# Hybrid attention and mixture kernel on one core: normalised tokens turned by DMA transposes instead of TensorE

## The chip, the cores and the metric

One core of a Trainium2 chip runs the whole program. The metric is the device time of one execution in microseconds (us), median of several runs. The engines are TensorE (PE for its matmuls, PEld for its weight loads), VectorE (DVE), ScalarE (ACT), GpSimd (POOL) and SyncE (SP), which only issues DMAs here.

## The reference

Four layers follow one another on x of shape (2, 2048, 256), each reading a layernorm of x and adding its result to x:

```python
x = x + attn_a(layernorm(x))   # 16 heads of 16, causal softmax attention, q = k = v = the normalised tokens
x = x + ffn(layernorm(x))      # router: mean over the tokens of a batch @ Wr, best 2 of 8 experts
x = x + attn_b(layernorm(x))   # q, k, v projections; scores = exp(-|q-k|^2); softmax(scores) @ v @ Wo
x = x + ffn(layernorm(x))      # same weights as the first ffn
# ffn: out = sum over the 2 chosen experts of weight * (gelu(h @ W1 + b1) @ W2 + b2), F = 1024
```

## The kernel before

x stays in SBUF as 32 tiles of 128 tokens by 256 features, tokens on partitions. A product with float32 accuracy is made of three fp16 products (`split_product`: high by high, high by low, low by high), so every operand is held as two fp16 halves, "high" and "low".

Both mixtures and the distance attention need the normalised tokens with features on partitions. The class `Columns` makes them in **units** of two tiles. There are 48 units: 0 to 15 for the first mixture, 16 to 31 for the distance attention, 32 to 47 for the second mixture. In a stage they are counted from that stage's base; in the distance attention this count is called p. For a unit, VectorE writes the normalised tokens in float32 (`norm`, c_xn), TensorE turns them with four float32 transposes into a PSUM bank (`turn`), ScalarE reads the bank for the high half (`high`, c_xhi), and VectorE reads it for the low half (`low`, c_xlo). Only units 0 and 1 take both halves on VectorE (`high_vector`). A ring of four units holds the result.

Every engine runs its own queue in program order, and the queues meet at semaphores. The stages:

- **Head attention** (to about 520 us). Steps of one or two "units" of scores; ACT takes exp of each. PE turns each finished output (`turn_out`) after VectorE has copied it out of PSUM (`copy_out`). VectorE's extra work is listed by output number i; LAST is the first output of the last head group. At i == LAST + 1 it finds the scales (`scales.finish`) and then runs `copy_out(i)`; at LAST + 3 it normalises units 0 and 1 and makes their halves.
- **Mixture** (`mixture`, run twice): 8 chunks of 512 tokens, 16 steps each (2 experts of 8 slices), 128 steps. A step n is `up(n)`, six matmuls of 512 columns on PE into f_h; gelu on ACT; the two halves f_hh and f_hl on VectorE; and, three steps later, `down(n)`, twelve matmuls of 256 columns. Side work is listed by step in `beside(n)`, identically for all engines: with c the chunk and a the step in it, the two units of the next chunk are normalised, turned and split at a = 7 to 9 and 10 to 12. `up` of a chunk's first step waits for that chunk's units. In chunk 0 the weights' halves are made along the way, one part a step, and `up(4)` waits for part 4.
- **Distance attention** (`distance_attention`): 8 chunks of 16 steps, 128 steps. A step is `scores(n)` (six matmuls of 512), d_dist on VectorE, two exp on ACT, the halves d_phi and d_plo on VectorE and `weighted(n - 4)` (twelve matmuls of 256). The table `AT` lists side work by step: norm, turn, values, project, lengths.
- SP issues loads: in a mixture the second batch's expert weights once its router has chosen (step 37), and in the last mixture the stores of the result.

Of the kernel before, what the change touches and what calls it, by code (L numbers as in the profile page):

```python
# [39 lines left out]
P = 128  # L40
# [390 lines left out]
def head_attention(pr, block, distance_inputs, cols, weights, mix, moving, fixed):  # L431
# [8 lines left out]
    with ExitStack() as ctx:  # L440
# [104 lines left out]
        def _(sp):  # L545
# [25 lines left out]
            mix.load_weights(sp, 0, chosen, range(len(mix.PIECES)))  # L571

        @block.vector
        def _(dve):
# [93 lines left out]
            for i, (G, c) in enumerate(outputs):  # L668
# [130 lines left out]
        def _(pe):  # L799
# [7 lines left out]
            def last_group(at):  # L807
# [172 lines left out]
class Columns:  # L980

    RING = 4

    def __init__(self, pr, ctx):  # L990
        sb = pr.sb(ctx)
        self.pr = pr
        self.xn = sb("c_xn", [P, self.RING, D], F32)
        self.hi = sb("c_xhi", [P, KD, self.RING * 2 * P], F16)
        self.lo = sb("c_xlo", [P, KD, self.RING * 2 * P], F16)
        self.s_xn, self.s_turn, self.s_hi, self.s_lo = pr.sems("cols", "xn", "turn", "xhi", "xlo")
# [5 lines left out]
    def at(self, u):  # L1002
        return slice((u % self.RING) * 2 * P, (u % self.RING + 1) * 2 * P)

    def chunk(self, u):

        return slice((u % self.RING) * 2 * P, (u % self.RING) * 2 * P + CHUNK)

    def norm(self, dve, u):
        pr = self.pr  # L1010
        if u >= 2:
            dve.wait_ge(self.s_turn, u - 1)
        for i in range(2):
            b, t = divmod(2 * u % (NB * TILES) + i, TILES)
            dve.tensor_scalar(self.xn[:, (2 * u + i) % self.RING, :], pr.x[:, b * TILES + t, :], pr.mv[:, b, t, 0:1], pr.rstd[:, b, t:t + 1],  # L1015
                              ALU.subtract, ALU.mult).then_inc(self.s_xn, 1)
# [9 lines left out]
    def high(self, act, u, bank):  # L1026
        act.wait_ge(self.s_turn, u + 1)
        act.activation(self.hi[:, :, self.at(u)], bank.rearrange("p (k n) -> p k n", k=KD), ACT.Copy, scale=self.scale(u))\
           .then_inc(self.s_hi, 1)

    def high_vector(self, dve, u, bank):
        dve.wait_ge(self.s_turn, u + 1)
        dve.tensor_scalar(self.hi[:, :, self.at(u)], bank.rearrange("p (k n) -> p k n", k=KD), self.scale(u), None, ALU.mult)\
           .then_inc(self.s_hi, 1)

    def low(self, dve, u, bank):
        dve.wait_ge(self.s_hi, u + 1)
        dve.scalar_tensor_tensor(out=self.lo[:, :, self.at(u)], in0=bank.rearrange("p (k n) -> p k n", k=KD), scalar=self.scale(u),
                                 in1=self.hi[:, :, self.at(u)], op0=ALU.mult, op1=ALU.subtract).then_inc(self.s_lo, 1)
# [172 lines left out]
def mixture(mix, block, loaded, last_layer, finish_ahead, banks_read, tiles_read, all_read):  # L1212
# [6 lines left out]
    with ExitStack() as ctx:  # L1219
# [19 lines left out]
        steps = [(q, c, e, j) for q in range(NB) for c in range(CHUNKS) for e in range(TOPK) for j in range(FT)]  # L1239
        def beside(n):  # L1240
# [5 lines left out]
            if not (last_layer and last_batch and c == CHUNKS - 1):  # L1246
# [914 lines left out]
```

## Time and profile before

| | us |
|---|---|
| median of 3 runs | 1654.05 (1653.84 to 1654.17) |
| the profiled execution, its own time | 1654.1 |
| its span in the trace | 1652.4 |
| PE busy in the span | 1607.8 (97%) |
| VectorE busy | 1069.2 (65%) |
| ScalarE busy | 987.2 (60%) |
| GpSimd busy | 358.9 (22%) |

The span runs from the first to the last instruction of the trace. Busy times overlap, so they do not add up. A share near 100% says which engine may bound a stage; the waits say whether it does.

### The profile page before, as it was taken

What the parts mean: (1) busy time and instruction counts of PE and PEld (TensorE: products, weight loads), DVE (VectorE), ACT (ScalarE), POOL (GpSimd) and SP (SyncE); (2) the same over time, 40 slices, a digit from 0 to 9 for tenths busy, and PEclk for the clock granted to TensorE, in tenths of its full rate; (3) what the DMA queues carried; (4) which work ended last, traced back from release to release, by engine and by line L of the source; (5) the groups of instructions that cost most, each with busy time, mean ns of one, the idle gap of its engine ahead of it and who ended that gap; (6) DMA issues with size and microseconds to landing.
All of it is one profiled execution on the core that took longest, in us unless ns stands there. A gap on an engine that the chain in (4) does not pass through costs nothing.

```text
span 1652.4 us, 30850 instructions
## 1 busy us (share of the span) xinstructions
PE 1607.8 (97%) x11947; PEld 891.8 (54%) x11947; DVE 1069.2 (65%) x2159; ACT 987.2 (60%) x1260; POOL 358.9 (22%) x466
## 2 busy tenths in 40 slices
PE   6999999999999999999999999999999899999998
PEld 2222222222233666666675666666666566666666
DVE  7533454454335975785557688868898887576554
ACT  6999999999998433433336554555445443353332
POOL 3022122122021000000005445544444300000000
PEclk9999999999999999999999999999999999999999
DMA  4013235100030003000000000000000200300000
GB/s 135 20 28 115 77 116 166 23 15 17 20 110 1 1 1 103 1 1 1 1 1 1 1 1 2 1 1 2 1 1 27 77 1 1 128 13 14 13 13 26
DMA packets 44335, 52.92 MB, mean 32 GB/s; under 512 B 3664, under 2 KB 39071, under 8 KB 44191
## 3 DMA queue, kind: packets, MB, share of 16 engines
q1 hardware_dynamic: 44190, 50.96, 9.8%
q8 instruction: 96, 1.57, 0.4%
q14 instruction: 49, 0.39, 0.1%
HBM read 38.88 MB, written 4.19 MB: 26 GB/s over the span
## 4 chain that ended last, share of the span: by engine, by line
PE 66%; ACT 16%; issue 11%; DVE 6%; DMA 0%; POOL 0%; ACTq 0%; DVEq 0%; SPq 0%; POOLq 0%
ACT a_probs L781 15%; PE f_ypsum L1045 7%; PE f_ypsum L1046 7%; PE f_ypsum L1044 7%; PE f_h L1044 7%; PE f_h L1045 7%; PE f_h L1046 7%; PE a_out L539 4%; PE d_outs L1044 3%; PE d_outs L1046 3%; PE d_outs L1045 3%; PE d_banks L1044 2%; PE d_banks L1046 2%; PE d_banks L1045 2%; PE a_scores L919 2%
## 5 line engine op out<-in xcount | busy, mean ns | idle before, releaser
L781 ACT ACTIVATE a_probs<-a_scores 128x1024 f32<-128x1024 f32 x544 | 499.9, 1208 | 8.2 <-PE a_scores L919 8.1
L1395 ACT ACTIVATE f_gelu<-f_h,f_bcol,s_more 128x512 f32<-128x512 f32 x256 | 199.0, 778 | 398.0 <-PE f_h L1046 386.3
L539 PE MATMUL a_out<-a_probs,a_values 128*32 128x512 f32 (+3 forms) x2560 | 294.0, 540 | 6.6 <-ACT a_probs L781 5.6
L1450 DVE TENSOR_SCALAR f_hh<-f_gelu,f_gates_scaled 128x512 f16<-128x512 f32 x256 | 136.7, 534 | 196.7 <-ACT f_gelu L1395 195.8
L1904 ACT ACTIVATE d_score<-d_dist,d_nksq,s_more 128x512 f32<-128x512 f32 x128 | 104.1, 813 | 191.8 <-DVE d_dist L2055 190.0
L1045 PE MATMUL f_ypsum<-f_w,f_hh 128*128 128x256 f16 x768 | 209.3, 273 | 0.0
L1046 PE MATMUL f_ypsum<-f_w,f_hl 128*128 128x256 f16 x768 | 209.3, 273 | 0.0
L1044 PE MATMUL f_ypsum<-f_w,f_hh 128*128 128x256 f16 x768 | 209.3, 273 | 0.0
L1452 DVE SCALAR_TENSOR_TENSOR f_hl<-f_gelu,f_gates_scaled,f_hh 128x512 f16<-128x512 f32 x256 | 192.2, 751 | 9.1
L919 PE MATMUL a_scores<-a_moving,a_fixed 64*128 64x512 f16 (+3 forms) x1280 | 184.0, 354 | 9.6 <-ACT a_probs L781 3.7
L795 POOL TENSOR_SCALAR_AFFINE_SELECT a_probs<-a_probs 128x256 f32<-128x256 f32 (+1 forms) x224 | 98.6, 456 | 420.7 <-ACT a_probs L781 412.5
L1941 POOL TENSOR_TENSOR distance_raw<-distance_raw,d_p 128x512 f32<-128x512 f32 x112 | 146.3, 1306 | 178.4 <-ACT d_p L1879 178.2
L1469 POOL TENSOR_TENSOR x<-x,f_b_wide 128x256 f32<-128x256 f32 x64 | 52.9, 848 | 523.6 <-DVE c_xn L1015 523.5
L1044 PE MATMUL f_h<-c_xhi,f_w 128*128 128x512 f16 x384 | 145.6, 379 | 1.3 <-DVE f_w L1122 1.2
L1045 PE MATMUL f_h<-c_xlo,f_w 128*128 128x512 f16 x384 | 145.5, 379 | 0.0
L1046 PE MATMUL f_h<-c_xhi,f_w 128*128 128x512 f16 x384 | 145.5, 379 | 0.0
L919 PEld LDWEIGHTS a_scores<-a_moving,a_fixed 64*128 64x128 f16 x1280 | 49.0, 94 | 173.3 <-ACT a_probs L781 118.7
L1045 PE MATMUL d_outs<-d_vlo,d_phi 128*128 128x256 f16 x512 | 139.6, 273 | 0.0
L1046 PE MATMUL d_outs<-d_vhi,d_plo 128*128 128x256 f16 x512 | 139.6, 273 | 0.0
L1044 PE MATMUL d_outs<-d_vhi,d_phi 128*128 128x256 f16 x512 | 139.6, 273 | 0.0
L618 DVE COPY a_moving<-a_out 128x1024 f16<-128x1024 f16 x31 | 21.4, 692 | 141.5 <-PE a_out L867 141.4
L539 PEld LDWEIGHTS a_out<-a_probs,a_values 128*32 128x32 f32 x2560 | 55.5, 108 | 96.0 <-issue 71.6
(271 smaller groups left out, 2737.9 us busy)
## 6 DMA issues: line engine op xcount, KB each, us to landing
f_raw<-in_L_ffn_W SPq DMA_DIRECT2D x16, 1024.0 KB, 7.6
f_raw<-in_L_ffn_W SPq DMA_DIRECT2D x24, 512.0 KB, 8.8
a_fixed<-a_moving SPq DMA_DIRECT2D x60, 96.0 KB, 2.3
x<-in_L_attn_a_x SPq DMA_DIRECT2D x7, 512.0 KB, 6.0
out<-x SPq DMA_DIRECT2D x7, 512.0 KB, 2.9
f_raw<-in_L_ffn_W SPq DMA_DIRECT2D x12, 256.0 KB, 4.0
a_fixed<-a_moving SPq DMA_DIRECT2D x60, 32.0 KB, 2.0
f_early_raw<-in_L_ffn_W SPq DMA_DIRECT2D x4, 256.0 KB, 3.4
```

Of the source, the lines that this page charges most:

```text
L539: mm = pe.matmul(spare[32 * j:32 * j + 32, i % 2, skip:skip + w], values[:, G % 2, kt + tile, j, :], probs[:, u % UR, j % 2, col:col + w], ...
L781: act.activation(probs[:, u % UR], scores[:, 2 * (u % SR):2 * (u % SR) + 2, :], ACT.Exp, scale=HD ** -0.5)\
L795: pool.affine_select(out=tri, in_=tri, compare_op=ALU.is_ge, fill=0.0, base=0, pattern=[[0, tri.shape[1]], [1, P]], channel_multiplier=-1) ...
L919: mm = pe.matmul(scores[:, 2 * (u % SR) + h, col_of[a]:col_of[a] + w], fixed[G % 2][head, a, k0:k0 + P], moving[G % 2][head, a, q0:q0 + w] ...
L1044: pe.matmul(out, fixed_hi, moving_hi, start=first, stop=False, skip_group_check=shared)
L1045: pe.matmul(out, fixed_hi, moving_lo, start=False, stop=False, skip_group_check=shared)
L1046: return pe.matmul(out, fixed_lo, moving_hi, start=False, stop=last, skip_group_check=shared)
L1395: act.activation(gel[:, n % HR, :], hps[:, n % 2, :], ACT.Gelu, bias=mix.bcol[:, q, FT * e + j:FT * e + j + 1], scale=pr.scales.hidden)\
L1450: dve.tensor_scalar(hh[:, n % HR, :], gel[:, n % HR, :], gate, None, ALU.mult).then_inc(s_hh, 1)
L1452: dve.scalar_tensor_tensor(out=hl[:, n % HR, :], in0=gel[:, n % HR, :], scalar=gate, in1=hh[:, n % HR, :], op0=ALU.mult, op1=ALU.subtract) ...
L1904: act.activation(score[:, n % 2, :], dist[:, n % DR, :], ACT.Exp, scale=pr.scales.distance, bias=nksq[:, b, kt:kt + 1]).then_inc(s_score, 1)
L1941: pool.tensor_tensor(acc, acc, p32[:, n % R, :], ALU.add).then_inc(s_acc, 1)
```

## The change

The four PE transposes of a unit go away. VectorE still writes the normalised tokens; ScalarE now reads these, untransposed in SBUF, for the high half, VectorE for the low half; then SP issues two DMA transposes, one for each half, each of a 128 by 512 fp16 tile in four blocks of 128 by 128. The ring grows from four to eight units. The columns are stored as tile, feature half, token, so that the 512 moving columns of a matmul are four runs of 128, 256 elements apart, where they were one run of 512. Users wait for the DMA's semaphore (`turned`).

The order of work changes with it. In a mixture the side work becomes norm, high, low at steps 1 to 3, 6 to 8 and 11 to 13 of a chunk, two units for each of chunks 0 to 3 and three for each later one; the first mixture thereby also makes the first six units of the distance attention. In the distance attention, units p = 6 and 7 are made at steps 0 to 4, and p = 8 to 12 from step 34 on. Units 0 and 1 are made on VectorE at i == LAST + 1, ahead of `copy_out`. Core of the diff:

```diff
+            for u in range(2):
+                cols.turn(sp, u)                # SP, head attention, behind load_weights
...
                     scales.finish(dve, spare[:, 0, :])
+                    for u in range(2):
+                        cols.norm(dve, u)
+                        cols.high_vector(dve, u)
+                        cols.low(dve, u)
                 if i == LAST + 2:
...
                 if i == LAST + 3:
-                    cols.norm(dve, 0)
-                    cols.norm(dve, 1)
                     mix.gate(dve, 0)
-                    for u in range(2):
-                        cols.high_vector(dve, u, spare[:, 0, :])
-                        cols.low(dve, u, spare[:, 0, :])
...
-                elif at in (26, 28):
-                    free(0)
-                    cols.turn(pe, (at - 26) // 2, spare[:, 0, :])
-                    reads[0].append((cols.s_lo, (at - 26) // 2 + 1))
...
-    RING = 4
+    RING, PARTS = 8, 2
...
-        self.hi = sb("c_xhi", [P, KD, self.RING * 2 * P], F16)
+        self.tokens_hi = sb("c_tokens_hi", [P, 4, D], F16)
+        self.hi = sb("c_xhi", [P, self.RING * 2, KD, P], F16)
...
-    def turn(self, pe, u, bank):
-        pe.wait_ge(self.s_xn, 2 * u + 2)
-        out = bank.rearrange("p (k n) -> p k n", k=KD)
-        for i in range(2):
-            for k in range(KD):
-                mm = pe.transpose(out[:, k, i * P:(i + 1) * P], self.xn[:, (2 * u + i) % self.RING, k * P:(k + 1) * P], self.pr.ident[:])
-        mm.then_inc(self.s_turn, 1)
+    def high(self, act, u):
+        act.wait_ge(self.s_xn, 2 * u + 2)
+        if u >= 2:
+            self.turned(act, u - 2)
+        act.activation(self.tokens_hi[:, self.place(u), :], self.xn[:, self.place(u), :], ACT.Copy, scale=self.scale(u))\
+           .then_inc(self.s_hi, 1)
...
+    def low(self, dve, u):
         dve.wait_ge(self.s_hi, u + 1)
+        if u >= 2:
+            self.turned(dve, u - 2)
+        dve.scalar_tensor_tensor(out=self.tokens_lo[:, self.place(u), :], in0=self.xn[:, self.place(u), :], scalar=self.scale(u),
+                                 in1=self.tokens_hi[:, self.place(u), :], op0=ALU.mult, op1=ALU.subtract).then_inc(self.s_lo, 1)
+
+    def turn(self, sp, u):
+        sp.wait_ge(self.s_lo, u + 1)
+        for to, of in ((self.hi, self.tokens_hi), (self.lo, self.tokens_lo)):
+            sp.dma_start(to[:, self.tile(u, 0):self.tile(u, 2)].rearrange("p t k n -> p (t k) n"),
+                         of[:, self.place(u), :].rearrange("p t d -> p (t d)"), transpose=True).then_inc(self.s_col[u % 2], 16)
+
+    def turned(self, engine, u):
+        engine.wait_ge(self.s_col[u % 2], 16 * self.PARTS * (u // 2 + 1))
...
+        def units_in(chunk):
+            first, count = (2 * chunk + 2, 2) if chunk < CHUNKS else (3 * chunk - 2, 3)
+            return [u for u in range(first, first + count) if u < TILES or not last_layer]
...
-                for f, i in {7: 0, 10: 1}.items():
-                    if f <= a <= f + 2:
-                        work.append((("norm", "turn", "low")[a - f], base + (TILES // 2) * q + 2 * (c + 1) + i))
+            for f, u in zip((1, 6, 11), units_in(CHUNKS * q + c)):
+                if f <= a <= f + 2:
+                    work.append((("norm", "high", "low")[a - f], base + u))
...
+            for chunk in range(NB * CHUNKS):    # SP in a mixture
+                for u in units_in(chunk):
+                    turn(u)
+                if chunk == CHUNKS // 2:
+                    chosen = mix.chosen(sp, 1, routing)
+                    mix.load_biases(sp, 1, chosen)
+                    mix.load_weights(sp, 1, chosen, range(len(mix.PIECES)))
+                if last_layer and chunk >= 1:
+                    store((chunk - 1) * TPC, TPC)
...
-            turn(2)                             # PE, start of the distance attention
             free_ahead(pe)
-            turn(3)
```

## Rows read from the trace of the kernel before

**Rows 1.** The profile page: busy us, share of the span, instructions of each engine.

```profile
PE 1607.8 (97%) x11947; PEld 891.8 (54%) x11947; DVE 1069.2 (65%) x2159; ACT 987.2 (60%) x1260; POOL 358.9 (22%) x466
```

**Rows 2.** Busy time by stretch: length, engines, clock (1.00 full), DMA share, GB/s.

```profile
478.00:495.00 17.00, 17.00 (x124) 5.57 (x123) 6.58 (x13) 14.54 (x17) 3.34 (x7) 1.00 0.25 86
520.00:862.00 342.00, 341.11 (x2376) 229.98 (x2377) 240.12 (x470) 128.56 (x178) 32.15 (x41) 1.00 0.04 13
862.00:1300.00 438.00, 429.36 (x2925) 287.10 (x2924) 356.74 (x655) 231.70 (x363) 200.02 (x164) 1.00 0.01 4
1190.00:1240.00 50.00, 48.10 (x329) 31.46 (x327) 49.41 (x78) 22.66 (x34) 20.18 (x17) 1.00 0.00 1
1310.00:1652.40 342.40, 336.04 (x2344) 229.29 (x2342) 226.19 (x413) 123.51 (x170) 23.36 (x28) 1.00 0.10 33
```

**Rows 3.** Timeline of PE around one turn: start, us, instruction.

```profile
543.97 0.60 PE L1023 MATMUL f_side<-ident,c_xn 128*128 128x128 f32 x4
544.40 0.38 PE L1044 MATMUL f_h<-c_xhi,f_w 128*128 128x512 f16 x1
544.62 0.38 PE L1045 MATMUL f_h<-c_xlo,f_w 128*128 128x512 f16 x1
```

**Rows 4.** Instructions that read c_xn on PE: ns min/median/max, first and last start.

```profile
L1023 PE MATMUL f_side<-ident,c_xn x120: 272/273/273, 544.0 to 1591.0; 128*128 128x128 f32 x120
...
L1023 PE MATMUL d_turns<-ident,c_xn x60: 272/273/328, 872.5 to 1243.6; 128*128 128x128 f32 x60
...
L1023 PE MATMUL d_banks<-ident,c_xn x4: 272/272/273, 872.1 to 872.4; 128*128 128x128 f32 x4
```

**Rows 5.** End of the head attention: timelines of DVE and ACT, one line of the chain.

```profile
476.37 0.69 DVE L626 COPY a_osb<-a_out 128x512 f32<-128x512 f32 x1
...
478.00 0.59 PE a_out L890 x4
...
479.85 0.48 DVE L1551 TENSOR_SCALAR wq_hi<-distance_raw,s_more 128x512 f16<-128x512 f32 x1
...
481.03 0.48 DVE L1551 TENSOR_SCALAR wk_hi<-distance_raw,s_more 128x512 f16<-128x512 f32 x1
...
494.89 5.61 ACT L781 ACTIVATE a_probs<-a_scores 128x1024 f32<-128x1024 f32 x6 [1.69 <-PE a_scores L919]
...
501.74 1.38 DVE L1015 TENSOR_SCALAR c_xn<-x,mv,rstd 128x256 f32<-128x256 f32 x4
```

**Rows 6.** Start of the first mixture: part 4 of the weights on DVE, up(4) on PE.

```profile
530.13 0.74 DVE L1122 SCALAR_TENSOR_TENSOR f_w<-f_raw,s_all,f_w 128x512 f16<-128x512 f32 x1
...
530.93 0.39 PE L1044 MATMUL f_h<-c_xhi,f_w 128*128 128x512 f16 x1
```

**Rows 7.** The same place in the second mixture.

```profile
1311.18 0.75 DVE L1122 SCALAR_TENSOR_TENSOR f_w<-f_raw,s_all,f_w 128x512 f16<-128x512 f32 x1 [0.20 <-ACT f_w L1113]
...
1311.99 0.39 PE L1044 MATMUL f_h<-c_xhi,f_w 128*128 128x512 f16 x1 [1.24 <-DVE f_w L1122]
```

**Rows 8.** Start of the distance attention: chain (two lines), DVE, PE.

```profile
885.27 1.03 DVE c_xn L1015 x2
...
890.68 0.73 DVE c_xn L1015 x2
...
898.36 0.69 DVE L1038 SCALAR_TENSOR_TENSOR c_xlo<-d_turns,c_xhi 128x512 f16<-128x512 f32 x1 [0.82 <-ACT c_xhi L1028]
...
915.46 0.38 PE L1044 MATMUL d_outs<-c_xhi,wk_hi 128*128 128x512 f16 x1
```

**Rows 9.** DMA: the SP queue's packets and share; an SBUF-to-SBUF copy, us to landing.

```profile
q1 hardware_dynamic: 44190, 50.96, 9.8%
...
a_fixed<-a_moving SPq DMA_DIRECT2D x60, 96.0 KB, 2.3
```

**Rows 10.** Groups of ACT: high half from PSUM, and a like one from SBUF.

```profile
L1113 ACT ACTIVATE f_w<-f_raw,s_all 128x512 f16<-128x512 f32 x48 | 34.1, 711 | 4.2 <-DMA f_raw<-in_L_ffn_W 4.2
...
L1028 ACT ACTIVATE c_xhi<-f_side 128x512 f16<-128x512 f32 x30 | 17.9, 597 | 29.0 <-PE f_side L1023 29.0
```

More of the change, by code:

```diff
@@ L1371, in do @@
             def do(kind, what):
-                if kind == "turn":
-                    cols.high(act, what, side[:])
+                if kind == "high":
+                    cols.high(act, what)
                 elif kind == "tanh":
@@ L1629, in distance_attention @@
               25: [("lengths", 7)],
-              44: [("norm", 8)],
-              45: [("norm", 9)],
-              47: [("turn", 8)],
-              48: [("norm", 10)],
-              49: [("turn", 9)],
-              50: [("norm", 11)],
-              51: [("turn", 10)],
-              52: [("turn", 11)],
-              53: [("project", 8, 0), ("norm", 12)],
+              34: [("norm", 8)],
+              35: [("high", 8)],
+              36: [("low", 8)],
+              38: [("norm", 9)],
@@ L1639, in distance_attention @@
+              39: [("high", 9)],
+              40: [("low", 9)],
+              42: [("norm", 10)],
+              43: [("high", 10)],
+              44: [("low", 10)],
+              46: [("norm", 11)],
+              47: [("high", 11)],
+              48: [("low", 11)],
+              50: [("norm", 12)],
+              51: [("high", 12)],
+              52: [("low", 12)],
+              53: [("project", 8, 0)],
               54: [("values", 8), ("project", 8, 1), ("norm", 13)],
-              55: [("lengths", 8), ("project", 9, 0)],
@@ L1641, in distance_attention @@
-              56: [("values", 9), ("project", 9, 1)],
-              57: [("turn", 12), ("project", 10, 0), ("lengths", 9)],
+              55: [("lengths", 8), ("project", 9, 0), ("high", 13)],
+              56: [("values", 9), ("project", 9, 1), ("low", 13)],
+              57: [("project", 10, 0), ("lengths", 9)],
               58: [("values", 10), ("project", 10, 1), ("norm", 14)],
-              59: [("turn", 13), ("lengths", 10), ("project", 11, 0)],
-              60: [("values", 11), ("project", 11, 1), ("norm", 15)],
@@ L1646, in distance_attention @@
-              61: [("turn", 14), ("project", 12, 0), ("lengths", 11)],
-              62: [("values", 12), ("project", 12, 1)],
-              63: [("turn", 15), ("lengths", 12)],
-              64: [("values", 13), ("project", 13, 0)],
+              59: [("lengths", 10), ("project", 11, 0), ("high", 14)],
+              60: [("values", 11), ("project", 11, 1), ("low", 14)],
+              61: [("project", 12, 0), ("lengths", 11)],
+              62: [("values", 12), ("project", 12, 1), ("norm", 15)],
@@ L1658, in distance_attention @@
               105: [("norm", 16)],
-              106: [("norm", 17)],
-              107: [("turn", 16)],
-              109: [("turn", 17)],
+              106: [("high", 16)],
+              107: [("low", 16)],
+              109: [("norm", 17)],
+              110: [("high", 17)],
+              111: [("low", 17)],
               117: [("tanh",)],
@@ L1724, in _ @@
         def _(sp):
+            free_ahead(sp)
+            for p in range(6, TILES + 2):
+                if p >= cols.RING:
+                    sp.wait_ge(s_v, p - cols.RING + 1)
+                    g = (p - cols.RING) // 2
+                    sp.wait_ge(s_p, KD * (max(task["q", g], task["k", g]) + 1))
+                cols.turn(sp, BASE + p)
             chosen = mix.chosen(sp, 0, routing)
@@ L1886, in weights_high @@
                 mix.part_high(act, 0, i)
-            do = {"turn": high, "values": values_high, "project": project_high, "tanh": tanh, "weights": weights_high}
+            do = {"high": high, "values": values_high, "project": project_high, "tanh": tanh, "weights": weights_high}
             act.activation(rden[0:1, 0, 0:1], pr.ones[0:1, 0:1], ACT.Exp).then_inc(s_table, 1)
@@ L1953, in _ @@
                         add_squares(what[0])
-                    if kind == "norm" and what[0] < BASE:
+                    if kind in ("add", "norm") and what[0] < BASE:
                         add_bias(what[0])
@@ L1963, in low @@
             def low(p):
-                cols.low(dve, BASE + p, turn_bank("turn", p))
+                cols.low(dve, BASE + p)
             def values_low(p):
```

133 lines of the change are left out of this document (58 added, 75 removed).

## The prediction

> **What bounds the kernel now.** I began with the page: PE is busy 97% of the span, no other engine above 65% [rows 1]. An average over stages doesn't say what a PE instruction is worth, so next I read busy time by stretch [rows 2]. In the first mixture PE is busy 341.1 of 342 us, in the second 336.0 of 342.4 including its tail; VectorE is at 70% and 66% there. In the distance attention PE has 429.4 of 438. The clock is full everywhere. Third, the timeline around a turn, to see whether PE's work there is back to back: the four transposes start at 543.97, the next matmul at 544.40 and the one after at 544.62 [rows 3], so a turn takes 0.43 us out of PE's stream (the 0.60 of its row overlaps its neighbour). What PE does not have to do in these stretches comes off the time. There are two exceptions. In 1190 to 1240 VectorE is busy 49.4 of 50 us and PE waits, but no turn lies in it. And the head attention mostly goes by ACT's exp, with one stretch, 478 to 495, in which PE is busy 17.0 of 17.0 us and ACT only 14.5 [rows 2]: there a stall of PE is lost time.
>
> **Removed from PE.** The turns are counted from the transposes [rows 4]: 120 + 60 + 4 = 184, four to a turn, so 46 turns after 520 us (16 in the first mixture, 16 in the distance attention, 14 in the second). 46 x 0.43 = 19.8 us. The two turns of the head attention lie beside ACT's exp and are worth nothing. Two places need a look. The 2 turns of steps 107 and 109 come behind the stretch where VectorE is the bound, and PE waits at times in steps 3 to 7 of the distance attention, where 4 turns lie; if neither gave anything, 6 x 0.43 = 2.6 us less would be saved.
>
> **Added on ACT and VectorE in the steady steps.** ACT's high half read PSUM in 597 ns; a like operation from SBUF takes 711 [rows 10]: 0.11 more, on an engine busy 128.6 of 342 us [rows 2], so nothing. VectorE's low half stays a two-input pass over 128x512; it moves within queues that have a quarter to spare. ACT no longer waits for PE's turn but for the norm, which is one step earlier. Hidden, unless VectorE is more than about one step late.
>
> **Moved: units 0 and 1 on VectorE, ahead of a copy.** This is the cost I find in the queues. At LAST + 1 the new block stands between `scales.finish` and `copy_out`. Before, the copy starts at 476.37, right behind the scales, takes 0.69, and PE's `turn_out`, which waits for it, starts at 478.00 [rows 5], 0.94 after the copy's end. The block: two norms of a unit cost half of 1.38, so 0.69 a unit; a high and a low half from SBUF take 1.18 (from wq_hi at 479.85 to wk_hi at 481.03) [rows 5]. 2 x (0.69 + 1.18) = 3.7 us. Queued behind it are `copy_out` and `finish_out` on VectorE; PE waits for the copy, 3.7 - 0.94 = 2.8 us, and behind PE's wait stand the products and scores that ACT needs. From 478 PE is the bound until ACT is fed again at 494.89, after waiting 1.69 [rows 5], and from there ACT is; so the stall passes to the end. Bounds: 0 if PE finds slack that busy time hides, 3.7 if none of the 0.94 covers it. I take +2.8. What is saved at LAST + 3 lies in VectorE's idle time.
>
> **Moved: the first unit's norm to step 1 of a chunk.** In chunk 0 of both mixtures it now stands before part 4 of the weights in VectorE's queue, and `up(4)` waits for that part. First mixture: part 4 is made at 530.13 in 0.74 and PE starts at 530.93 [rows 6], so there is no slack; a norm (0.65 to 0.73 for two tiles) delays PE by 0.65. Second mixture: part 4 starts at 1311.18 after 0.20 idle and PE has waited 1.24 for it [rows 7]; 0.65 - 0.20 = 0.45 more. Together +1.1 (bounds 0 and 1.4). Later steps of chunk 0 have VectorE catching up, so nothing more.
>
> **Added: 96 DMA transposes.** No transfer before is a transpose. Nearest below: an SBUF-to-SBUF copy of 96 KB lands in 2.3 us [rows 9]. By packets: 9.8% of 16 engines' span for 44190 packets is 0.059 us each [rows 9]; 128 partitions by 4 blocks as packets of 256 bytes are 512 packets, 512 x 0.059 / 16 = 1.9 us. Two transposes of a unit then take T = 2 x 1.9 + 2.3 = 6 us. If instead every 2-byte element were a packet, one transpose would take 65536 x 0.059 / 16 = 240 us. I take 6, since the copy row is the nearest. The cover: in a mixture a step is 342 / 128 = 2.7 us, less the turns 2.6; a chunk's second unit has its low half at step 8 and is needed at step 16, about 21 us. `high` and `low` wait for the transposes of two units ago, ten steps. SP has little else; the second batch's weights now wait behind unit 7 (steps 38 to 41) and are not used before step 56. The tightest place is p = 7 in the distance attention: its low half comes in step 4, where before unit p = 5 had it at 898.36, and `project` needs it where PE stood at 915.46 [rows 8], less four removed turns, 913.7. That is 15 us for one T. p = 6 is split in step 2, some 1.5 us behind the 890.68 row, so both must fit into 913.7 - 892.2 = 21.5 us: T up to 10.7 costs nothing.
>
> The Trainium skill (VectorE: DVE Perf Modes, The three transpose paths) gives 1309 ns for a DMA transpose of 128x128; eight blocks one after another are by that page 10.5 us, an estimate, which would leave the sum as it is. No row here shows it.
>
> **Start of the distance attention.** VectorE and ACT carry the chain here, with c_xn at 885.27 (1.03) and 890.68 (0.73) in it [rows 8]. Four of six units go elsewhere, but what remains is packed into steps 0 to 4, with norms, a low half and POOL's adds earlier. I see up to 3 us either way, and count only PE's turns.
>
> **Sum.** -19.8 + 2.8 + 1.1 = -15.9 us. The profiled execution took 1654.1, of which 1652.4 is span; it stands at the median of the runs (1654.05). 1654.1 - 15.9 = **1638.2 us**, 1.0% faster.
>
> **Rivals.**
>
> 1. *The stall at LAST + 1 does not reach the end, or the distance start gains more.* For: the four units that leave that chain. Against: PE at 17.0 of 17.0. Worth 2.8 to 5.8 less: 1632.5 to 1635.5.
>
> 2. *The transposes come too late: slower.* Place: p = 7. Over T = 13.9 us, three units a chunk of 16 x 2.61 = 41.8 us no longer fit, and the backlog of twelve units from chunk 4 on meets p = 6 and 7. Chunk 4 starts four chunks before the mixture's end at 867.1, so at 699.9; the first low half is 7.8 us later; p = 7 lands at 707.7 + 14 T and is due at 913.7. The loss is 14 T - 206 us. It cancels the gain of 15.9 from T = 15.8; with T = 20 it is 74 us: 1712. For it: no row shows a transpose, and element-wise packets would be far beyond. Against: the copy row.
> The Trainium skill's same page (Rules for kernel authors) says to transpose 128x128 on TensorE if PSUM will do as a destination; by that rule the change would be for the worse, and this rival is how.
>
> 3. *The moving operand in four runs of 128 columns slows the matmuls.* 1536 + 192 = 1728 matmuls read it, one each 0.216 us (544.40 to 544.62). No matmul of before reads separated runs. 9 ns each cancel the gain; doubling them would cost 373 us. Against: the transposes, 128 columns each, come at 0.43 / 4 = 0.11 us, and a break is no new instruction.
>
> 4. *No change:* removed turns uncover other waits. VectorE is at 81% in the distance attention [rows 2]; if none of its 16 turns paid and the other costs stood at their bounds, 30 x 0.43 = 12.9 less 5.1 would still be 7.8 us faster. Same time needs some of rival 2 or 3 as well.
>
> **How the numbers follow.** Forecast 0.62 (own range 1635 to 1643); rival 1, 0.17; between the forecast and no gain, 1643 to 1651, 0.06; no change to 0.2%, about 3.3 us, which is about what a measurement of this kernel can tell, 0.03; rival 2, 0.08; rival 3, 0.04. Faster 0.85, same 0.03, slower 0.12. The range 1632 to 1650 leaves out the slower cases and a little below: about 2 in 10.
>
> **What the profile after would show.** No c_xn on PE; PE's matmul of 512 columns still each 0.216 us; first mixture about 6.9 - 0.65 us shorter, the second 6.0 - 0.45; a wait of PE's a_out transpose for a_osb of about 3 us near 478; DMA transposes landing in about 4 us, and PE never waiting for one. Wrong would be: waits of PE or ACT for a transpose, above all at the start of the distance attention; longer matmuls; or an unchanged distance stage with VectorE near 100%.

## The result, and the profile after

The changed kernel takes 1646.52 us (median of 6 runs, 1646.32 to 1648.1) against 1654.11 us for the kernel before (6 runs, 1652.36 to 1654.31). The ratio is 0.996, 95% interval 0.9948 to 0.9972: 0.4% faster, where 1.0% (1638.2 us) was forecast. The runs of either kernel fall on two levels some 1.8 us apart, five of the six of before on the upper one and four of the six after on the lower, so that within a level the change gains some 6 us and not 7.6, and where the medians of a few runs are compared below, 1.8 us are not told from chance.

The profile page of the changed kernel, the line that answers to [rows 1]:

```profile
PE 1589.9 (97%) x11755; PEld 869.9 (53%) x11755; DVE 1079.5 (66%) x2159; ACT 985.9 (60%) x1260; POOL 360.7 (22%) x466
```

The turns are gone: 192 fewer matmuls, 17.9 us less of PE. But the span fell by 7.8 us only (1652.4 to 1644.6), and VectorE has 10.3 us more to do in the same number of instructions. That second number was not in the forecast. Busy time by stretch, answering to [rows 2] (length, engines, granted clock, DMA share, GB/s):

```profile
478.00:484.00 6.00, 5.14 (x28) 1.02 (x28) 4.34 (x10) 2.33 (x4) 0.00 (x0) 0.72 1.27 220
...
520.00:862.00 342.00, 340.16 (x2364) 226.73 (x2363) 248.36 (x488) 134.39 (x187) 35.25 (x45) 1.00 0.12 29
862.00:1300.00 438.00, 422.83 (x2846) 278.11 (x2845) 365.01 (x643) 228.03 (x356) 202.56 (x164) 1.00 0.05 11
1000.00:1040.00 40.00, 38.34 (x263) 25.03 (x262) 39.52 (x56) 20.17 (x31) 21.70 (x19) 1.00 0.14 27
1230.00:1255.00 25.00, 21.84 (x152) 14.19 (x151) 24.62 (x35) 12.02 (x20) 11.55 (x8) 1.00 0.12 23
```

To see where the time went I set the two traces side by side by TensorE's own landmarks: the first matmul of a step of the mixture or of the distance attention, and in the head attention ACT's exp of a unit. A stretch between two landmarks holds the same work in both kernels. All in us:

| landmark | before | after | this stretch, after less before | forecast |
|---|---|---|---|---|
| exp 500 of the head attention | 478.26 | 476.33 | -1.93 | 0 |
| exp 510 | 487.76 | 490.24 | **+4.42** | +2.8 |
| mixture 0, last step | 860.40 | 856.90 | -5.99 | -6.9 + 0.65 |
| distance attention, step 8 | 911.55 | 904.72 | -3.33 | -2.6 |
| step 42 | 1017.27 | 1010.44 | 0 | 0 |
| step 72 | 1134.66 | 1129.72 | **+1.89** | -3.4 |
| step 108 | 1238.00 | 1233.09 | +0.03 | 0 |
| step 114 | 1254.74 | 1252.39 | **+2.57** | -0.9 |
| mixture 1, last step | 1640.58 | 1632.83 | -5.41 | -6.0 + 0.45 |

The column of forecasts adds to -15.9, the measured one to -7.75. The -1.93 at the top is older than anything that was changed: the granted clock of 20 to 30 us is 0.83 in the profiled run of before and 1.00 in the one after (1.00 is 2.4 GHz and a stretch at 1.2 GHz counts half). The change itself is worth the other 5.8 us. The two rows, first before, then after:

```profile
20.00:30.00 10.00, 8.06 (x84) 2.73 (x74) 6.94 (x19) 6.39 (x8) 3.52 (x7) 0.83 0.19 49
```

```profile
20.00:30.00 10.00, 9.03 (x102) 3.12 (x99) 8.25 (x28) 8.98 (x10) 3.31 (x7) 1.00 0.23 59
```

Three rows in bold hold the miss: the stall is 1.6 us dearer than forecast, and the two stretches of the distance attention together are 8.8 us worse. There units p = 8 to 17 are made: 8 to 15 in steps 34 to 64, and 16 and 17, the first two of the second mixture, in steps 105 to 111.

**The stall.** The waits of PE in 476 to 490, and PE's timeline behind the wait:

```profile
PE a_out L887 <- DVE a_osb L628: 2.8, 1, 2.8
```

```profile
478.86 0.66 PE L887 MATMUL a_out<-ident,a_osb 128*128 128x128 f32 x4 [2.78 <-DVE a_osb L628]
479.45 1.68 PE L539 MATMUL a_out<-a_probs,a_values 128*32 128x512 f32 x8
```

The wait is the forecast's 2.8 us to the tenth. What it did not have stands behind it: the granted clock is 0.72 in 478 to 484, where it was 1.00 before, and the 8 products take 1.68 us. The same 8 before:

```profile
478.52 1.07 PE L539 MATMUL a_out<-a_probs,a_values 128*32 128x512 f32 x8
```

**The distance attention.** In 1000 to 1040 VectorE is busy 39.52 of 40 us and PE 38.34; in 1230 to 1255 it is 24.62 and 21.84 of 25. The same lines of the kernel before, for 1000 to 1040 and 1235 to 1260:

```profile
1000.00:1040.00 40.00, 40.00 (x280) 27.30 (x279) 33.03 (x55) 19.96 (x31) 23.44 (x20) 1.00 0.00 1
1235.00:1260.00 25.00, 24.97 (x179) 16.93 (x178) 23.32 (x43) 13.41 (x21) 12.30 (x9) 1.00 0.01 2
```

So the bound moved from TensorE to VectorE. PE's waits for VectorE in 980 to 1260, first before, then after, say the same:

```profile
PE d_banks L1044 <- DVE d_dist L2055: 1.8, 4, 0.8
```

```profile
PE d_banks L1047 <- DVE d_dist L2070: 4.7, 10, 0.8
PE d_misc L396 <- DVE pooled L390: 1.8, 1, 1.8
PE d_outs L1047 <- DVE x L2031: 1.2, 1, 1.2
```

Why VectorE is longer is seen by groups; first after, then before, both 980 to 1260, VectorE (busy us, mean ns | idle before):

```profile
L2015 DVE TENSOR_SCALAR d_phi<-d_p 128x512 f16<-128x512 f32 x86 | 54.3, 631 | 0.0
...
L1032 DVE SCALAR_TENSOR_TENSOR c_tokens_lo<-c_xn,c_tokens_hi 128x512 f16<-128x512 f32 x10 | 13.6, 1362 | 0.0
L1013 DVE TENSOR_SCALAR c_xn<-x,mv,rstd 128x256 f32<-128x256 f32 x20 | 12.9, 687 | 0.0
```

```profile
L1996 DVE TENSOR_SCALAR d_phi<-d_p 128x512 f16<-128x512 f32 x87 | 50.7, 583 | 0.0
...
L1015 DVE TENSOR_SCALAR c_xn<-x,mv,rstd 128x256 f32<-128x256 f32 x20 | 10.5, 565 | 0.0
...
L1038 DVE SCALAR_TENSOR_TENSOR c_xlo<-d_turns,c_xhi 128x512 f16<-128x512 f32 x10 | 6.9, 690 | 3.0 <-ACT c_xhi L1028 3.0
```

The low half went from 690 to 1362 ns. It is the same operation on as many elements; its float32 input went from PSUM (`d_turns`) to SBUF (`c_xn`). It is not slow by itself: over the whole kernel its minimum and median are 680 and 684 ns, its maximum 1760. Timelines of VectorE and GpSimd side by side show what the long ones have in common:

```profile
1022.74 1.76 DVE L1032 SCALAR_TENSOR_TENSOR c_tokens_lo<-c_xn,c_tokens_hi 128x512 f16<-128x512 f32 x1
```

```profile
1022.61 1.33 POOL L1960 TENSOR_TENSOR distance_raw<-distance_raw,d_p 128x512 f32<-128x512 f32 x1 [0.80 <-ACT d_p L1900]
```

GpSimd's sum of the softmax denominators began at 1022.61 and ended at 1023.94, 1.20 us after the low half's start; the low half took 1.76 and ended 0.56 us behind it. In the distance attention ten low halves begin under a GpSimd instruction, and nine of them end 0.55 us behind its end. The tenth, at 887.75, took 0.68; there GpSimd's add of a bias took 1.43 us, the longest of its 32 (median 0.83). Passes with one input in SBUF are held too where they write fp16 from float32 (`d_phi`, up to 1.49 us for 0.42) or normalise (`c_xn`, up to 1.37 for 0.40), but not the statistics of x (0.42 at most). The kernel before had a low half and such a sum side by side too, and nothing happened:

```profile
1035.56 0.69 DVE L1038 SCALAR_TENSOR_TENSOR c_xlo<-d_turns,c_xhi 128x512 f16<-128x512 f32 x1 [0.23 <-ACT c_xhi L1028]
```

```profile
1035.12 1.33 POOL L1941 TENSOR_TENSOR distance_raw<-distance_raw,d_p 128x512 f32<-128x512 f32 x1 [0.80 <-ACT d_p L1879]
```

**The transposes** are waited for by nobody. They land in 2.4 and 2.5 us (median), and no wait of PE or ACT ends with one:

```profile
c_xhi<-c_tokens_hi SPq DMA_TRANSPOSE x48, 2.4
c_xlo<-c_tokens_lo SPq DMA_TRANSPOSE x48, 2.5
```

### The profile page after: what moved, and what is told of

Same layout as the page of the kernel before. It is cut to its first block, busy times and chain, and to the rows that moved or that the text cites. A ratio compares the mean times of both kernels' runs of the same rounds, so it can differ in the third digit from the quotient of the medians.

```text
span 1644.6 us, 30645 instructions
## 1 busy us (share of the span) xinstructions
PE 1589.9 (97%) x11755; PEld 869.9 (53%) x11755; DVE 1079.5 (66%) x2159; ACT 985.9 (60%) x1260; POOL 360.7 (22%) x466
## 4 chain that ended last, share of the span: by engine, by line
PE 63%; ACT 16%; issue 11%; DVE 8%; POOL 1%; DMA 0%; ACTq 0%; DVEq 0%; POOLq 0%
ACT a_probs L782 15%; PE f_ypsum L1047 7%; PE f_ypsum L1049 7%; PE f_ypsum L1048 7%; PE f_h L1047 7%; PE f_h L1049 7%; PE f_h L1048 7%; PE a_out L539 4%; PE d_outs L1047 3%; PE d_outs L1049 2%; PE d_outs L1048 2%; PE a_scores L916 2%; DVE d_dist L2070 2%; PE d_banks L1047 2%; PE d_banks L1049 2%
```

## The experiments

The lengths of the stretches, each less that of the kernel before, from each kernel's profiled run (us):

| kernel | start to exp 500 | exp 500 to 510 | mixture 0 | distance 34 to 72 | 72 to 108 | 108 to 114 | 114 to mixture 1 | mixture 1 | span |
|---|---|---|---|---|---|---|---|---|---|
| after | -1.93 | +4.42 | -5.99 | +1.89 | +0.03 | +2.57 | 0.00 | -5.41 | 1644.6 |
| a1 units 0, 1 put back | -0.01 | 0.00 | -6.00 | +1.87 | +0.03 | +2.56 | +1.67 | -5.42 | 1643.8 |
| a2 one unit ahead | -0.24 | +1.00 | -5.99 | +1.84 | +0.01 | +2.55 | 0.00 | -5.42 | 1642.8 |
| a3 weights first | -0.13 | +4.42 | -6.05 | +1.82 | +0.02 | +2.57 | -0.01 | -4.99 | 1646.7 |
| e1 steps 7, 10, 13 | -0.17 | +4.43 | -6.71 | +1.88 | +0.02 | +2.56 | +1.63 | -6.03 | 1646.7 |
| b4 old steps | -0.34 | +4.42 | -5.99 | +2.29 | -0.01 | +1.60 | 0.00 | -5.42 | 1645.6 |
| b1 GpSimd narrow | -1.23 | +4.41 | -5.99 | -2.55 | -3.68 | -0.47 | -3.22 | -5.41 | 1630.8 |
| b2 the same, before | -1.66 | +0.01 | 0.00 | -0.03 | -3.24 | -0.03 | -3.23 | +0.24 | 1644.4 |
| b3 low half narrow | -2.09 | +2.84 | -5.99 | -0.57 | +0.02 | +1.62 | +1.67 | -5.41 | 1641.1 |
| c1 units 8 to 17 by TensorE | -1.71 | +4.41 | -5.99 | -0.02 | +0.01 | 0.00 | +3.31 | -5.42 | 1643.6 |
| d0 new steps, SBUF | -1.87 | +4.26 | -5.99 | +5.95 | +0.05 | +2.56 | +1.69 | -5.41 | 1650.3 |
| d1 new steps, PSUM | -1.62 | +4.38 | -5.99 | -0.11 | -0.68 | -0.30 | 0.00 | -5.41 | 1639.3 |
| f1 all three | -1.63 | +0.01 | -6.62 | -0.11 | -0.69 | -0.29 | +1.67 | -5.59 | 1635.8 |

The start of the distance attention up to step 34 is left out: -3.3 to -3.4 in every kernel with the change. Stretches that an edit doesn't touch repeat to a few hundredths, apart from the first, the stall and the one behind step 114: there the granted clock falls in some executions and not in others.

### a1: units 0 and 1 back in their old place

```diff
                     scales.finish(dve, spare[:, 0, :])
-                    for u in range(2):
-                        cols.norm(dve, u)
-                        cols.high_vector(dve, u)
-                        cols.low(dve, u)
...
                 if i == LAST + 3:
+                    cols.norm(dve, 0)
+                    cols.norm(dve, 1)
                     mix.gate(dve, 0)
+                    for u in range(2):
+                        cols.high_vector(dve, u)
+                        cols.low(dve, u)
```

> Against the changed kernel (1646.5 us), with VectorE's work for units 0 and 1 put back behind the copy_out of LAST + 2, where it stood before the change. Theory 1: the 4.4 us that TensorE loses between probability units 500 and 510 come whole from this block (2.8 us of waiting for a_osb, and some 1.6 us at half the granted clock behind the wait): 4.4 us faster, 1642.1 us, the granted clock stays at 1.0 there and no wait of 2.8 us for a_osb is left. Rival, the linear one that the prediction used: only the wait of 2.8 us goes, 1643.7 us. Rival: what comes free here is waited for again at the first up-projection of mixture 0, since the transposes of units 0 and 1 then start later: 0 us, and a wait for c_xlo at mixture 0's start.

Measured 1644.54 us (4 runs, 1643.52 to 1645.46; ratio to before 0.9946, 0.9929 to 0.9962). The stretch is back at 0.00 and its clock at 1.00, so all 4.42 us belong to the block. The time moved by 2.0 us, not the 4.4 expected. The profiled run pays 1.67 us at the end of the distance attention, where PE waits 1.5 and 2.1 us for VectorE's gates; the changed kernel has the same two waits at full clock, this run fell to 0.72 behind them. The first stretch is 1.92 us longer than in the profiled run of after as well.

```profile
PE d_misc L1207 <- DVE gathered L1203: 2.1, 1, 2.1
PE d_misc L1187 <- DVE f_gates_scaled L1183: 1.5, 1, 1.5
```

```profile
1286.00:1292.00 6.00, 5.53 (x23) 2.90 (x24) 4.00 (x8) 2.67 (x4) 1.53 (x3) 0.72 0.01 4
```

### a2: one unit ahead instead of two

```diff
-                    for u in range(2):
+                    for u in range(1):
                         cols.norm(dve, u)
                         cols.high_vector(dve, u)
                         cols.low(dve, u)
...
                 if i == LAST + 3:
+                    cols.norm(dve, 1)
+                    cols.high_vector(dve, 1)
+                    cols.low(dve, 1)
                     mix.gate(dve, 0)
```

> Only unit 0 stands ahead of the copy_out of LAST + 1, unit 1 behind that of LAST + 2. The block is then some 1.85 us against a slack of 0.94 us. Theory 1 (the clock falls because the wait is long): a wait of about 0.9 us and no fall of the clock, so that units 500 to 510 cost +0.9 us against the kernel before, 3.5 us less than in the changed kernel: 1643.0 us. Rival, linear: half of the loss stays, +2.2 us, 1644.3 us. Rival: the loss has nothing to do with the length of the block: +4.4 us, 1646.5 us.

Measured 1644.53 us (one run). PE's wait for `a_osb` is 1.0 us, the clock stays at 1.00, and the stretch costs +1.00. Half of the block is 1.87 us by the prediction's own rows, less the slack of 0.94 leaves 0.93: the linear count is right for the wait. The rest of the 4.42 is the clock, and another run shows it apart: in b3, whose head attention is that of the changed kernel, PE waited the same 2.8 us, the clock stayed at 1.00, and the stretch cost +2.84.

```profile
PE a_out L890 <- DVE a_osb L628: 1.0, 1, 1.0
```

```profile
478.00:484.00 6.00, 5.28 (x42) 1.58 (x44) 4.20 (x10) 5.33 (x7) 0.00 (x0) 1.00 1.26 284
```

The same window and the wait in b3:

```profile
478.00:484.00 6.00, 5.29 (x42) 1.59 (x44) 4.18 (x10) 3.50 (x5) 0.00 (x0) 1.00 1.18 203
```

```profile
PE a_out L887 <- DVE a_osb L628: 2.8, 1, 2.8
```

### a3 and e1: the mixtures' units behind the weights, or at the old steps

a3 moves the three lines in `beside` that append norm, high and low below the one that appends the weights. e1 is:

```diff
-            for f, u in zip((1, 6, 11), units_in(CHUNKS * q + c)):
+            for f, u in zip((7, 10, 13), units_in(CHUNKS * q + c)):
```

> In the mixtures' side work the norm, the high half and the low half of a unit stand behind the weights' halves of the same step, in place of ahead of them. Theory 1: the +0.99 us at steps 3 to 6 of mixture 0 and the +0.7 us at the start of mixture 1 are weights that VectorE and ScalarE make later by the length of a norm and a high half: both vanish, 1.7 us faster than the changed kernel, 1644.8 us. Rival: they are the transfers of the transposes, or SP's queue, which this leaves alone: 0 us, 1646.5 us.

> The changed kernel with the units of a mixture chunk taken up at its steps 7, 10 and 13 instead of 1, 6 and 11. Theory: the +0.99 us at steps 3 to 6 of mixture 0 and the +0.49 us at the start of mixture 1 come from the norm and high half at steps 1 to 3, beside the making of weights that the next up-projections wait for: both vanish, 1.5 us faster, 1645.0 us. Rival: the transposes, having less lead, are waited for at the next chunk: over 1646.5 us.

a3 measured 1648.39 us and e1 1648.37 us (one run each; in both the first stretch is 1.8 us longer than in the profiled run of after, and e1 lost 1.63 us behind step 114). By the stretches, a3 is 0.06 us better in mixture 0 and 0.42 worse in mixture 1, and e1 gains 0.72 and 0.62, 1.3 us of the expected 1.5. Step by step more can be seen. `up(4)` starts 0.79 us late in mixture 0 of the changed kernel and 0.49 late in mixture 1, both against the kernel before, behind the norm and part 4 in VectorE's queue:

```profile
532.29 0.73 DVE L1013 TENSOR_SCALAR c_xn<-x,mv,rstd 128x256 f32<-128x256 f32 x2
...
533.27 0.88 DVE L1125 SCALAR_TENSOR_TENSOR f_w<-f_raw,s_all,f_w 128x512 f16<-128x512 f32 x1
```

```profile
534.21 0.39 PE L1047 MATMUL f_h<-c_xhi,f_w 128*128 128x512 f16 x1 [0.80 <-DVE f_w L1125]
```

In a3, with part 4 ahead of the norm, it is 0.00 and 0.19: the order is the cause of this part. But a3 pays it back. `up(6)`, which loses 0.20 in either mixture of the changed kernel, loses 0.59 in a3 (its wait is below), and some 0.35 more is lost before step 12. At steps 7, 10 and 13 (e1) neither `up(4)` nor `up(6)` of mixture 0 is late at all.

```profile
541.02 0.39 PE L1047 MATMUL f_h<-c_xhi,f_w 128*128 128x512 f16 x1 [0.43 <-DVE f_w L1125]
```

### b1 and b2: GpSimd's sums narrowed, after and before

```diff
                     pool.wait_ge(s_acc, added[0])
-                    pool.tensor_tensor(acc, acc, p32[:, n % R, :], ALU.add).then_inc(s_acc, 1)
+                    some = slice(0, 64)
+                    pool.tensor_tensor(acc[:, some], acc[:, some], p32[:, n % R, some], ALU.add).then_inc(s_acc, 1)
```

> The changed kernel with GpSimd's accumulation of the softmax denominators narrowed from 512 to 64 columns (but for the first one of each chunk): it leaves out seven eighths of the denominators' sums. Theory 2a: VectorE's passes whose operands all lie in SBUF are stretched while GpSimd works on SBUF. Then c_tokens_lo falls from 1.25 us to about 0.7 us, VectorE is no longer the bound, and the 8.9 us missing in steps 43 to 63 and 109 to 114 come back: 1637.6 us. Rival 2b: the low half is long for its own sake (two float operands out of SBUF): it stays at 1.25 us and the time at 1646.5 us.

> The same cut of GpSimd's accumulation in the kernel before (it leaves out seven eighths of the denominators' sums). Its low halves read PSUM and TensorE is its bound there. Theory 2a: no change beyond 1 us, 1654.1 us, which makes the gain of the changed kernel's twin its own. Rival: GpSimd's accumulation is itself something that the distance stage waits for, and both kernels gain alike.

b1 measured 1632.52 us, b2 1646.14 us (one run each). In the two stretches of units 8 to 17 the changed kernel goes from +4.46 to -3.02, 7.5 us of the 8.8 that were missing; the kernel before doesn't move there (-0.06). The low half:

```profile
L1032 DVE SCALAR_TENSOR_TENSOR c_tokens_lo<-c_xn,c_tokens_hi 128x512 f16<-128x512 f32 x10 | 7.7, 767 | 0.0
```

1362 to 767 ns with not one instruction of VectorE changed. The edit frees the other passes over SBUF too, so the 7.5 us are not the low half's alone. Both kernels also win in 72 to 108 and behind 114, b1 6.9 us against the change and b2 6.5 against the kernel before, where the expectation had put at most 1 us and only its rival had both gain. Up to step 108 VectorE is the bound in 1190 to 1240 [rows 2], and passes over SBUF are held there as well: `d_phi` takes 611 ns in 72 to 108 of the kernel before and 416 in b2. Behind 114 PE waits for VectorE, first before, then in b2 (1250 to 1300):

```profile
PE d_misc L1203 <- DVE gathered L1199: 2.2, 1, 2.2
PE d_misc L1183 <- DVE f_gates_scaled L1179: 1.5, 1, 1.5
```

```profile
PE d_misc L1203 <- DVE gathered L1199: 0.4, 1, 0.4
```

The kernel before had been paying this all along.

### b3: the low half of units 8 to 17 over 64 of 512 columns

```diff
+        part = slice(0, 32 if 24 <= u < 34 else D)
-        dve.scalar_tensor_tensor(out=self.tokens_lo[:, self.place(u), :], in0=self.xn[:, self.place(u), :], scalar=self.scale(u),
+        dve.scalar_tensor_tensor(out=self.tokens_lo[:, self.place(u), part], in0=self.xn[:, self.place(u), part], scalar=self.scale(u),
```

> The changed kernel with the low half of units 8 to 17 of the distance stage made over 64 of 512 columns (it leaves out seven eighths of those low halves); transposes, norms and high halves are left as they are. Theory 2: 1.1 us of VectorE are gone for each of ten units, TensorE is the bound again, and 8.9 us come back: 1637.6 us. Rival: the missing time lies in the transposes (SP, DMA) or in ScalarE's extra 0.6 us for the high half, which all stay: 1646.5 us.

Measured 1642.83 us (one run). 3.4 us come back in the two stretches (+4.46 to +1.05), not the 8.9 expected. The group says why: with an eighth of the columns it still takes 897 ns.

```profile
L1033 DVE SCALAR_TENSOR_TENSOR c_tokens_lo<-c_xn,c_tokens_hi 128x64 f16<-128x64 f32 x10 | 9.0, 897 | 0.0
```

One of the ten began with GpSimd idle and took 215 ns; five took 1291 to 1293. What lengthens it is a wait inside the instruction, whose size does not depend on its own. So an estimate of VectorE's load by elements, mine of 1.1 us saved for a unit included, is wrong here.

### b4: units 8 to 17 at the steps of the kernel before

The rows of the table `AT` for these units are those of the kernel before, each turn replaced by a high and a low half.

> The changed kernel with units 8 to 17 of the distance stage taken up at the steps of the kernel before (norms at 44, 45, 48, 50, 53, 54, 58, 60, 105, 106, both halves at 47, 49, 51, 52, 57, 59, 61, 63, 107, 109), still turned by DMA. Theory 2: in the distance stage VectorE is the bound because its low half (c_xn and c_tokens_hi, both in SBUF) takes 1.25 us where the old one (PSUM) took 0.69 us. Then putting the units closer together helps nothing: between 2 us slower and 1 us faster than the changed kernel, and the low halves still take over 1.1 us. Rival (the placement is at fault, not the length): the 8.9 us that are missing in steps 43 to 63 and 109 to 114 come back, 1637.6 us. Rival (DMA lead): TensorE waits for columns at its projections of steps 53 to 61, and the time is over 1650 us.

Measured 1647.3 us (one run). The two stretches together cost +3.89 instead of +4.46. When the units are taken up makes 0.6 us here. The low halves still take 1324 ns, as expected.

### c1: units 8 to 17 by TensorE again, the others by DMA

```diff
+    def turn_pe(self, pe, u, bank, s_turn):
+        pe.wait_ge(self.s_xn, 2 * u + 2)
+        out = bank.rearrange("p (t k n) -> p t k n", t=2, k=KD)
+        for i in range(2):
+            for k in range(KD):
+                mm = pe.transpose(out[:, i, k, :], self.xn[:, 2 * (u % 2) + i, k * P:(k + 1) * P], self.pr.ident[:])
+        mm.then_inc(s_turn, 1)
```

with both halves reading the bank, at the old steps.

> The changed kernel with units 8 to 17 of the distance stage turned by TensorE into PSUM as before, at the steps of the kernel before, their halves read from the bank; all other units are turned by DMA. Theory 2: these ten units cost 4.35 us of TensorE's turns and win back the 8.9 us: the ledger of steps 42 to 114 is that of the kernel before, 4.5 us faster than the changed kernel, 1642.0 us. Rival: the loss is not tied to where the low half reads: the turns of TensorE come on top, 1650.9 us.

Measured 1644.65 us (4 runs, 1643.74 to 1645.39; ratio to before 0.9945, 0.9929 to 0.9962). Steps 42 to 114 are those of the kernel before to 0.02 us, 4.5 us better than the change. At the end of the distance attention 3.31 us go again, by the same waits and a clock of 0.91 and then 0.68 in the two windows from 1280. Handing these ten units to the DMA queues, with their tokens in SBUF, was worth less than nothing.

### d1 and d0: the normalised tokens in PSUM, and their control

d1 leaves every transpose to the DMA queues and writes the norms of units 8 to 17 into the bank of the values, at steps 33 to 52 (and 105 to 111), where that bank is free. d0 has the same steps with the tokens in `c_xn`.

```diff
+    def rows(self, u):
+        if u in self.IN_BANK:
+            return self.bank.rearrange("p (t d) -> p t d", t=2)
+        return self.xn[:, self.place(u), :]
...
-            dve.tensor_scalar(self.xn[:, 2 * (u % 2) + i, :], pr.x[:, b * TILES + t, :], pr.mv[:, b, t, 0:1], pr.rstd[:, b, t:t + 1],
+            dve.tensor_scalar(self.rows(u)[:, i, :], pr.x[:, b * TILES + t, :], pr.mv[:, b, t, 0:1], pr.rstd[:, b, t:t + 1],
```

> The changed kernel, its transposes all left to the DMA queues, with the normalised tokens of units 8 to 17 of the distance stage written into the PSUM bank of the values instead of c_xn, so that both halves read PSUM; their steps move to 33 to 52, where that bank is free. Theory 2, sharpened by the traces of the narrowed kernels: a VectorE pass whose operands all lie in SBUF and that begins while GpSimd's tensor_tensor runs is held to its end; one with an operand in PSUM is not. Then the low half takes 0.69 us whatever GpSimd does, and with TensorE's turns gone too the 8.9 us missing after step 42 come back: 1637.6 us by the changed kernel's level. Rival (the two norms of a unit, 0.64 us each by the mean, are held as well and are as much to blame): about half comes back, 1642 us. Rival (ScalarE or SP): 1646.5 us.

> The control of the last: the same steps 33 to 52, the normalised tokens in c_xn in SBUF as in the changed kernel. Theory 2: the low halves are held by GpSimd again (1.1 to 1.8 us) and steps 33 to 53 are at least 3 us longer than with the tokens in PSUM: 1644 to 1648 us. Rival (the steps were at fault): the same time as with the tokens in PSUM.

d1 measured 1642.72 us (4 runs, 1641.02 to 1644.49; ratio to before 0.9936, 0.992 to 0.9953), d0 1651.98 us (one run). From step 34 to 114 d1 is at -1.09 and d0 at +8.56: 9.6 us between two kernels that differ in the place of one tile (and in one wait of the norms that goes with it). d0 is 4.1 us worse than the changed kernel in these stretches and above the 1644 to 1648 that was expected: packing the units closer made the loss larger, which b4's 0.6 us had not shown. First d1, then d0, VectorE in 980 to 1260:

```profile
L1022 DVE TENSOR_SCALAR d_turns<-x,mv,rstd 128x256 f32<-128x256 f32 x20 | 9.9, 541 | 0.1
L1041 DVE SCALAR_TENSOR_TENSOR c_tokens_lo<-d_turns,c_tokens_hi 128x512 f16<-128x512 f32 x10 | 6.8, 679 | 0.0
```

```profile
L1041 DVE SCALAR_TENSOR_TENSOR c_tokens_lo<-c_xn,c_tokens_hi 128x512 f16<-128x512 f32 x10 | 15.4, 1542 | 0.0
```

Against the changed kernel d1 wins 5.6 of the 8.8 us, not all: VectorE is still busy 39.41 of 40 us in 1000 to 1040, where d_phi and the other passes over SBUF are held as before, and a norm into PSUM takes 541 ns where one into SBUF takes some 404 undisturbed. How the missing 3.2 us divide between these was not tested. The measured time is that of the rival in the expectation (about half comes back, 1642 us), but not by its mechanism: the norms into PSUM are not held (548 ns at most).

### f1: a1, e1 and d1 together

> Together: units 0 and 1 behind the copy_out of LAST + 2, the mixtures' units at steps 7, 10 and 13, the distance stage's units 8 to 17 through the PSUM bank. If the three are independent: 4.4 + 1.5 + 8.9 = 14.8 us less than the changed kernel, 1631.7 us, faster than both. If the pause of TensorE at the end of the distance stage falls so that the granted clock drops behind it, as it did with units 0 and 1 put back, 1633.4 us. Rival: gains in the distance stage are taken back by waits at its end: 1637 us or more.

Measured 1637.07 us (4 runs, 1634.99 to 1637.5; ratio to before 0.9894, 0.9878 to 0.9911): 17.0 us faster than the kernel before and 9.5 us faster than the change. By stretches 4.4 us come from the stall, 0.63 and 0.18 from the mixtures and 5.6 from the distance attention; the second mixture gives less than the 0.62 of e1, and the distance attention less than the 8.9 that I had put in, as in d1. So 1637.07 is 5.4 us above the expected 1631.7 and at the time of its rival; 3.3 us of that are d1's smaller part. The profiled run pays 1.67 us behind step 114.

## Why the prediction was wrong

The time came out between the forecast and no gain, where the prediction had put a chance of 0.06, and of its signs of being wrong one is there: VectorE near 100% with the distance stage about as long as before (1.2 us longer by the table, for 6.9 forecast shorter).

**What held.** The price of a turn: mixture 0 lost 16 turns and 6.98 us between steps 6 and 127, against 6.9. The wait for `a_osb`: 2.8 us. The transposes: 2.4 and 2.5 us to landing, inside the 6 us taken for a unit and well under the 10.5 us that the prediction estimated for eight blocks one after another; rival 2 is out. ScalarE's high half takes 0.62 us from SBUF, 0.02 more than from PSUM, not 0.11. The matmuls over four runs of 128 columns keep their cadence of 0.216 us; rival 3 is out. The start of the distance attention, -3.33 against -2.6: my "up to 3 us either way" contained it. Rival 1 is out in its first half: the stall reached the end in full (a1).

**What failed: "Added on ACT and VectorE in the steady steps".** The prediction put it thus: the low half "stays a two-input pass over 128x512; it moves within queues that have a quarter to spare. Hidden". Both halves of that are wrong where the distance attention is concerned. The pass went from a PSUM operand to two in SBUF, and with GpSimd at work it took 1362 ns instead of 690 (the norms 687 instead of 565). And the quarter to spare was an average over the mixtures; in the distance attention it was 19%, and those 356.7 of 438 us [rows 2] hold stretches in which VectorE was full already, and in 1000 to 1040, where units 8 and on are taken up now, it had 33.03 of 40. Cost: 5.3 us in steps 42 to 72 and 3.5 in 108 to 114, 8.8 us where the whole sum missed the profiled span by 8.1; the other rows nearly cancel. b1 shows it from GpSimd's side (7.5 us come back, all passes freed), and d0 and d1 from the operand's (9.6 us at the same steps). Against the changed kernel d1 wins back 5.6 of the 8.8; what the other 3.2 are made of is argued, not shown.

The Trainium skill (SBUF — State Buffer, Who interferes with whom) states this: VectorE and GpSimd share a pair of ports to SBUF, a VectorE instruction with two SBUF inputs contends with a GpSimd instruction that reads SBUF, as does a VectorE pass in one of the fast modes that use both pairs of ports, and whoever issues second is blocked until the first ends. The runs here agree: 1.76 us against 0.68 with both inputs in SBUF, and 0.69 us beside a GpSimd pass of 1.33 with one of them in PSUM. It bears on the low halves, and I had not weighed it.

**What was mis-sized: "units 0 and 1 on VectorE, ahead of a copy", +2.8.** It measured 4.42, and a1 shows that all of it is the block's. The wait was sized rightly (2.8, and 1.0 in a2); 1.6 us are the clock that fell behind it, and where it did not fall (b3) the stall cost 2.84. The upper bound of 3.7 counted VectorE's work alone and was too low.

**Small: the first unit's norm at step 1.** Against turns at 0.437 us, mixture 0 lost 1.0 us (16 x 0.437 = 6.99 less 5.99) and mixture 1 0.7 us (14 x 0.437 = 6.12 less 5.41), for 0.65 and 0.45. The mechanism I gave, the place ahead of part 4 in VectorE's queue, is borne out at `up(4)`: 0.79 and 0.49, and 0.00 and 0.19 in a3. What it did not have is the 0.20 at `up(6)` in either mixture; "nothing more" in later steps was wrong.

**Rival 4** was argued away with a floor: even if none of the distance attention's 16 turns paid, 7.8 us would be left. The profiled span fell by 7.8 us and so seems to meet the floor, but 1.93 of that is the clock of the first 30 us, which is luck. The 5.8 us of the change are 2 us under the floor: the stall cost 0.7 more than its bound of 3.7, the mixtures 0.1 more, and the distance attention, taken at nothing, cost 1.2. The floor assumed that a removed turn could be worth nothing, never less; ten of them, with their tokens in SBUF, were worth -4.5 us (c1).

## What to carry to other kernels

When a tile moves from PSUM to SBUF, price every VectorE pass that reads it again, and look at what GpSimd does in the same microseconds: here a pass with two inputs in SBUF that began under GpSimd's sums waited for their end, even when it needed only 0.2 us itself. Work that is taken off TensorE pays only in stretches where the next engine has room, so read the engine that takes it over by stretch and not by stage. And a wait on TensorE can cost more than its length, if the clock falls behind it: 2.8 us of waiting cost 4.3 to 4.4 here in eight of nine profiled executions, and 2.84 in the ninth.

## What was not expected of the hardware

- A low half over 64 columns took 897 ns with GpSimd at work, more than the undisturbed 684 ns over 512 columns; undisturbed it took 215.
- GpSimd's sums cost the kernel before some 6.5 us (b2), in stretches in which it looked like a mere spectator at 22% of the span.
- The granted clock falls behind one and the same wait in some executions and not in others: 0.72 behind 2.8 us in the changed kernel, 1.00 in b3; and the two waits of 1.5 and 2.1 us in front of the last steps of the distance attention left it at 1.00 in the changed kernel and took it to 0.72 in a1. What decides is open. The first stretch varies in the same way: the granted clock of 20 to 30 us is 0.83 in six of the fourteen profiled executions, whose first stretch is within 0.34 us of that of before, and 1.00 in the other eight, where it is 1.2 to 2.1 us shorter.
- A DMA transpose of 128 x 512 two-byte elements lands in 2.4 to 2.5 us (5.6 and 6.4 at most), about the 2.3 us of a 96 KB copy before [rows 9].
